# Layer-norm transposes by DMA instead of TensorE, with the second normalization after the attention output

## What is computed

```python
# attention, on xn = layernorm(x)
q = softmax(xn @ Wq, axis=-1)
k = softmax(xn @ Wk, axis=-2)
v = xn @ Wv
ctx = (k.T @ v) / 8            # 1024 x 1024 per sequence
x = x + ((q @ ctx) / 1024) @ Wo + bo

# mixture of experts, on h = layernorm(x)
probs = sigmoid((h @ Wr) * routing_bias)        # 7 routed experts
scores, idx = top_k(probs, 2); scores /= scores.sum(-1)
out = shared_expert(h) + sum_e expert_e(h) * weight_e
expert(h) = (silu(h @ wg) * (h @ wu)) @ wd      # 1024 -> 2816 -> 1024
x = x + out
```

## Time and profile before

| | |
|---|---|
| device time, two timed runs | 4908.41 and 4373.74 us, median 4641.08 us |
| device time of the profiled execution | 4353.71 us |
| its span on the slowest core (core 5) | 4352.2 us |
| spans of all cores | 4312.2 to 4352.2 us |
| first expert matmul | 669.4 us |

### The profile page before, as it was taken

One profiled execution on the slowest core, in us unless ns is written; L12 is line 12 of the kernel. 1 busy time (PEld: TensorE's weight loads), 2 busy tenths in 40 slices (PEclk: granted clock), 3 DMA queues, 4 the chain that ended last, 5 costly groups with the idle time before them and its releaser, 6 DMA issues.

```text
span 4352.2 us, 48589 instructions; the slowest of 8 cores (4312.2 to 4352.2 us)
## 1 busy us (share of the span) xinstructions
PE 4134.2 (95%) x19072; PEld 1879.8 (43%) x19072; DVE 944.8 (22%) x1314; ACT 530.6 (12%) x930; POOL 235.8 (5%) x269
## 2 busy tenths in 40 slices
PE   5899548999999999999999999999999999999998
PEld 2344223444444444444444444444444444444443
DVE  2111331222222221212221222222222222122212
ACT  2211111011110101010101010101111010101010
POOL 1000220000000000000000000000000000000000
PEclk7789768999999999999999999999999999999999
DMA  6001104222130313131313131222222130213132
GB/s 121 24 0 25 49 20 66 37 39 42 26 55 15 55 21 49 30 51 27 53 23 54 27 49 32 44 37 39 42 35 46 17 63 15 47 29 49 27 54 78
DMA packets 83199, 175.64 MB, mean 40 GB/s; under 512 B 5024, under 2 KB 5024, under 8 KB 82976
## 3 DMA queue, kind: packets, MB, share of 16 engines
q0 software_dynamic: 76288, 147.36, 21.6%
q1 hardware_dynamic: 6688, 25.17, 1.8%
HBM read 310.94 MB, written 8.39 MB: 73 GB/s over the span
## 4 chain that ended last, share of the span: by engine, by line
PE 95%; DVE 2%; issue 1%; POOL 1%; ACT 1%; DMA 1%; DVEq 0%; POOLq 0%; ACTq 0%; SPq 0%
PE PS L520 28%; PE PS L529 28%; PE PS L554 14%; PE PS L556 14%; PE PS L273 2%; PE PS L248 1%; PE PS L374 1%; PE PS L454 1%; PE PS L456 1%; PE PS L301 1%; PE PS L297 1%; PE PS L295 1%; PE PS L299 1%; PE PS L323 1%; PE PS L325 1%
## 5 line engine op out<-in xcount | busy, mean ns | idle before, releaser
L520 PE MATMUL PS<-h2T,ring 128*128 128x512 bf16 x5632 | 1332.1, 379 | 10.9 <-DMA ring<-wgu 10.9
L529 PE MATMUL PS<-h2T,ring 128*128 128x512 bf16 x5632 | 1331.4, 379 | 0.0
L554 PE MATMUL PS<-wd_sb,hid 128*128 128x512 bf16 x2816 | 1067.2, 379 | 16.8 <-DVE hid L539 16.8
L556 PE MATMUL PS<-wd_sb,hid 128*128 128x512 bf16 x2816 | 1067.2, 379 | 0.0
L539 DVE TENSOR_TENSOR hid<-sg,PS 128x512 bf16<-128x512 bf16 x704 | 484.2, 688 | 1950.2 <-PE PS L529 1950.2
L520 PEld LDWEIGHTS PS<-h2T,ring 128*128 128x128 bf16 x5632 | 551.3, 98 | 676.2 <-issue 12.7
L529 PEld LDWEIGHTS PS<-h2T,ring 128*128 128x128 bf16 x5632 | 551.3, 98 | 665.6 <-issue 1.9
L536 ACT ACTIVATE sg<-PS 128x512 bf16<-128x512 f32 x704 | 420.5, 597 | 3165.1 <-PE PS L520 3165.0
L562 DVE SCALAR_TENSOR_TENSOR x<-PS,w_sb,x 128x1024 f32<-128x1024 f32 x224 | 287.6, 1284 | 801.3 <-PE PS L556 801.3
L554 PEld LDWEIGHTS PS<-wd_sb,hid 128*128 128x128 bf16 x2816 | 275.4, 98 | 354.8 <-issue 24.2
L556 PEld LDWEIGHTS PS<-wd_sb,hid 128*128 128x128 bf16 x2816 | 275.4, 98 | 330.3
(11 more groups left out here) (71 smaller groups left out, 821.4 us busy)
## 6 DMA issues: line engine op xcount, KB each, us to landing
ring<-wgu POOLq DMA_DIRECT2D x176, 512.0 KB, 5.4
wd_sb<-rdn POOLq DMA_DIRECT2D x14, 1536.0 KB, 15.1
wd_sb<-rdn POOLq DMA_DIRECT2D x14, 1280.0 KB, 16.5
xslot<-x SPq DMA_DIRECT2D x32, 512.0 KB, 3.7
out<-x SPq DMA_DIRECT2D x2, 4096.0 KB, 13.0
wd_sb<-sdn POOLq DMA_DIRECT2D x2, 1536.0 KB, 15.5
wd_sb<-sdn POOLq DMA_DIRECT2D x2, 1280.0 KB, 16.3
wq_sb<-wq POOLq DMA_DIRECT2D x1, 2048.0 KB, 22.6
```

What stands on the lines that cost most here:

```text
L520: last = te.matmul(PSUM[:, gb * 512:(gb + 1) * 512], ring[slot][:, 0, ic, :], h2T[:, ic, noff:noff + 512], start=(ic == 0), stop=(ic == NI ...
L529: last = te.matmul(PSUM[:, ub * 512:(ub + 1) * 512], ring[slot][:, 1, ic, :], h2T[:, ic, noff:noff + 512], start=(ic == 0), stop=(ic == NI ...
L554: last = te.matmul(PSUM[:, b0 * 512:(b0 + 1) * 512], lhs, wd_sb[wbuf][:, hcl, 0:512], start=st, stop=sp_)
L556: last = te.matmul(PSUM[:, b1 * 512:(b1 + 1) * 512], lhs, wd_sb[wbuf][:, hcl, 512:1024], start=st, stop=sp_)
```

## The change

- The eight TensorE transposes and two ScalarE evictions of `layernorm_transpose` are replaced by one DMA transpose on the SP queue, from the scratch tile straight into h1T or h2T. The scratch tiles become bf16. A resource, `xp_chain`, makes each transpose wait for the completion of the one before.
- In `layernorm_transpose` VectorE computes veps ahead of negm.
- The interleaved loop is taken apart: first the attention output for all 16 tiles, then `snap_a8` and the allocation of the expert buffers, then, in four blocks, the normalization of four tiles followed by the routing of four tiles.
- In `emit_routing` the last step, one operation with two multiplications, becomes two operations, and the banks are 4 and 5.

```diff
-    h1scr = alloc("h1scr", [128, D], F32, side="right")
+    h1scr = alloc("h1scr", [128, D], BF16, side="right")
...
+    xp_chain = Res()
...
+    s_xp = p.sem("s_xp")
...
         p.op("dve", lambda v: v.bn_aggr(mv[:], stat6[:]), reads=[stat_r], writes=[mv_r])
+        p.op("dve", lambda v: v.tensor_scalar(veps[:], mv[:, 1:2], EPS, None, ALU.add),
+             reads=[mv_r], writes=[veps_r])
         p.op("dve", lambda v: v.tensor_scalar(negm[:], mv[:, 0:1], -1.0, None, ALU.mult),
              reads=[mv_r], writes=[negm_r])
-        p.op("dve", lambda v: v.tensor_scalar(veps[:], mv[:, 1:2], EPS, None, ALU.add),
-             reads=[mv_r], writes=[veps_r])
...
              reads=[src_res, negm_r, rstd_r], writes=[scr_res])
-        for half in range(2):
-            bank = banks[half]
-
-            def tfn(te, half=half, bank=bank):
-                last = None
-                for q in range(4):
-                    ic = half * 4 + q
-                    last = te.transpose(PSUM[:, bank * 512 + q * 128: bank * 512 + (q + 1) * 128],
-                                        scr[:, ic * 128:(ic + 1) * 128], ident[:])
-                return last
-            p.op("pe", tfn, reads=[scr_res, ident_r], writes=[PS[bank]])
-
-            def efn(e, half=half, bank=bank, t=t):
-                dst = dstT[:, half * 4:(half + 1) * 4, t * 128:(t + 1) * 128]
-                src = PSUM[:, bank * 512:(bank + 1) * 512]
-                return e.activation(dst, src, AF.Copy)
-            p.op("act", efn, reads=[PS[bank]], writes=[dstT_res])
+        p.op("sp", lambda sp, t=t: sp.dma_start_transpose(
+            dstT[:, 0:8, t * 128:(t + 1) * 128], scr[:]),
+            reads=[scr_res, xp_chain], writes=[dstT_res, xp_chain],
+            sem=s_xp, inc=16)
...
-    def emit_routing(t, bank=None):
-        if bank is None:
-            bank = 4 if t % 2 == 0 else 5
+    for t in range(NT):
...
+    free("xb1"); free("xb0"); free("bo_bc"); free("wo_sb"); free("yT")
+    snap_a8 = p.snapshot()
...
+    def emit_routing(t):
+        bank = 4 if t % 2 == 0 else 5
...
+        p.op("dve", lambda v: v.tensor_scalar(wtmp[:, 0:NR], probs[:, 0:NR], minv[:],
+                                              None, ALU.mult),
+             reads=[probs_r, minv_r], writes=[wtmp_r])
...
-        p.op("dve", lambda v, t=t: v.scalar_tensor_tensor(
-            w_sb[:, t * 8: t * 8 + NR], probs[:, 0:NR], minv[:], maskb[:, 0:NR],
-            ALU.mult, ALU.mult),
-            reads=[probs_r, minv_r, mask_r], writes=[w_r])
...
-    h2scr = alloc("h2scr", [128, D], F32, side="right")
-    h2scr_r = Res(war0=snap_a7)
-
-    def emit_ln2_routing(t):
-        layernorm_transpose(t, x2[:, t * D:(t + 1) * D], x2_r[t], h2scr, h2scr_r,
-                            h2T, h2T_r[t // 4], banks=(4, 5) if t % 2 == 0 else (6, 7))
-        emit_routing(t, bank=7 if t % 2 == 0 else 5)
...
-        if t >= 2:
-            emit_ln2_routing(t - 2)
-    for t in (NT - 2, NT - 1):
-        emit_ln2_routing(t)
...
+        p.op("dve", lambda v, t=t: v.tensor_tensor(
+            w_sb[:, t * 8: t * 8 + NR], wtmp[:, 0:NR], maskb[:, 0:NR], ALU.mult),
+            reads=[wtmp_r, mask_r], writes=[w_r])
+
+
+    h2scr = alloc("h2scr", [128, D], BF16, side="right")
+    h2scr_r = Res(war0=snap_a8)
+    for blk in range(NT // 4):
+        for t in range(blk * 4, blk * 4 + 4):
+            layernorm_transpose(t, x2[:, t * D:(t + 1) * D], x2_r[t], h2scr, h2scr_r,
+                                h2T, h2T_r[t // 4], banks=(0, 1) if t % 2 == 0 else (2, 3))
+        for t in range(blk * 4, blk * 4 + 4):
+            emit_routing(t)
+    free("h2scr")
```

More of the change, by code:

```diff
@@ L466, in build_nc @@
             reads=[PS[b0], PS[b0 + 1], rsq_r, xb_r[sl]], writes=[x2_r[t]])
-        if t >= 2:
-            emit_ln2_routing(t - 2)
-    for t in (NT - 2, NT - 1):
-        emit_ln2_routing(t)
-    free("h2scr"); free("xb1"); free("xb0"); free("bo_bc"); free("wo_sb"); free("yT")
+    free("xb1"); free("xb0"); free("bo_bc"); free("wo_sb"); free("yT")
     snap_a8 = p.snapshot()
@@ L485, in build_nc, with lfn @@
     sg_r = [Res(war0=snap_a8), Res(war0=snap_a8)]
+    def emit_routing(t):
+        bank = 4 if t % 2 == 0 else 5
+        def lfn(te, t=t, bank=bank):
+            last = None
+            for ic in range(NI):
+                last = te.matmul(PSUM[:, bank * 512: bank * 512 + NR],
+                                 h2T[:, ic, t * 128:(t + 1) * 128],
+                                 wr_sb[:, ic, :], start=(ic == 0), stop=(ic == NI - 1))
+            return last
+        p.op("pe", lfn, reads=[h2T_r[t // 4], wr_r], writes=[PS[bank]])
+        p.op("dve", lambda v, bank=bank: v.tensor_tensor(
+            wtmp[:, 0:NR], PSUM[:, bank * 512: bank * 512 + NR], rb_bc[:], ALU.mult),
+            reads=[PS[bank], rb_r], writes=[wtmp_r])
+        p.op("act", lambda s: s.activation(maskb[:, 0:NR], wtmp[:, 0:NR], AF.Exp,
+                                           scale=-1.0),
+             reads=[wtmp_r], writes=[mask_r])
+        p.op("dve", lambda v: v.tensor_scalar(maskb[:, 0:NR], maskb[:, 0:NR], 1.0,
+                                              None, ALU.add),
+             reads=[mask_r], writes=[mask_r])
+        p.op("dve", lambda v: v.reciprocal(probs[:, 0:NR], maskb[:, 0:NR]),
+             reads=[mask_r], writes=[probs_r])
+        p.op("dve", lambda v: v.max(m8[:], probs[:]), reads=[probs_r], writes=[m8_r])
+        p.op("dve", lambda v: v.tensor_tensor(msum[:], m8[:, 0:1], m8[:, 1:2], ALU.add),
+             reads=[m8_r], writes=[msum_r])
+        p.op("dve", lambda v: v.reciprocal(minv[:], msum[:]), reads=[msum_r], writes=[minv_r])
+        p.op("dve", lambda v: v.tensor_scalar(wtmp[:, 0:NR], probs[:, 0:NR], minv[:],
+                                              None, ALU.mult),
+             reads=[probs_r, minv_r], writes=[wtmp_r])
+        p.op("dve", lambda v: v.tensor_scalar(maskb[:, 0:NR], probs[:, 0:NR], m8[:, 1:2],
+                                              None, ALU.is_ge),
+             reads=[probs_r, m8_r], writes=[mask_r])
+        p.op("dve", lambda v, t=t: v.tensor_tensor(
+            w_sb[:, t * 8: t * 8 + NR], wtmp[:, 0:NR], maskb[:, 0:NR], ALU.mult),
+            reads=[wtmp_r, mask_r], writes=[w_r])
```

## The result

| | before | after |
|---|---|---|
| device time | 4317 to 4318 us, one of 4374 | 4358 to 4366 us |
| ratio of device times, 95% interval | 1 | 1.0102, 1.0089 to 1.0114 |
| profiled execution's span, core 3 | 4312.2 us | 4361.5 us |

The changed kernel is 1.0% slower, about 44 us. Every kernel here also has executions that are up to hundreds of microseconds longer at a lower granted clock: they are left out of all device times and ratios, and where a kernel gave no other, the span of one of its cores at the usual clock is given instead.

The account below looks back on a forecast made before the run. Outside the TensorE-busy expert loop, chains through one tile were taken to bound the two changed pieces. First stage +84 and second -30 gave +54 on 4353.71, so 4408 us; range 4340 to 4540.

Parts of the forecast that it names:

- the base: The undisturbed time of the kernel before, to which the predicted difference was added: the profiled execution's 4353.71 us.
- T: Time from issue of a 128x1024 bf16 DMA transpose to its landing: taken as 5 us, between 2.6 and 14.8.
- the formula: Whole kernel's predicted difference, -70 + 12I + 20T: +54 us with I = 2 and T = 5.
- I: Time SP is held between issuing a transpose and issuing what is behind it: taken as 2 us, at least 0.33.
- within 2%: Whole kernel: time changes by less than 2%, about what a measurement was taken to tell from no change; chance 0.57.
- The x load loses its prefetch and lies on the chain: First normalization: the next x load queues behind the transpose on SP; a tile takes 8.2 + I = 10.2 us, not 4.83.
- First stage +84: First normalization and Q matmuls, four blocks: a loss of 40.4 + 12I + 4T = 84 us.
- Second stage -30: Attention output, second normalization and routing, up to the experts: a gain of 110.3 - 16T = 30 us.
- the 7.85 us wait: Before the experts: the wait for first expert weights, claimed covered by issuing them during the last transpose and routing.
- Attention output alone at 3.46 us a tile: Second stage's start: TensorE sets the pace without transposes, 16 x 3.46 = 55.4 us.
- The rival at 0.81: Attention output alone: runs at the lower clock or paced by POOL, 13 us more; inside the forecast's range, no separate chance.
- price of its small pieces: Each of 32 transposes pays per small piece: T = 10.5 gives 4534 us, T = 14.8 gives 4660; chance 0.38.

Follow-up runs that it names:

- e1: The changed kernel with each x load of the first normalization issued ahead of the transpose of the tile before: 4306 us, 0.9973 of before.
- e5: The kernel before, TensorE transposes kept, with each x load of the first normalization issued only once the tile before is normalized: 4372 us, 1.0127 of before.
- e7: The changed kernel with each transpose split into two DMA transposes of 512 columns, the second waiting for the first: core 1 spans 4419.6 us.
- e4: The changed kernel with the first expert weights issued only when the last transpose has landed: 4349 us, timed once.
- e6: The changed kernel with the loads of Wk and Wv issued only after the first four transposes have landed: core 1 spans 4347.0 us, no device time.
- e8: The kernel before with next-block normalization between Q matmuls (TensorE transposes) and a rearranged interleaved second stage with DMA transposes, first expert weights behind the last: 4196.6 us.
- e10: The kernel of e8 with msum, a sum of two 128x1 columns on VectorE, written as tensor_scalar instead of tensor_tensor: 4191.2 us, timed once.

## Why the prediction was right and where it was wrong

The forecast was 4408 us, the changed kernel takes 4361. Of the 47 us between them 36 are the base (item 9): against the 4318 us that the kernel before takes, the forecast says +90 where +44 was measured. The other 10 are the sum, +54 against +44. That it came so near is luck: its term T was 5 us where 3.07 was measured, which by the formula (20T) is 39 us too much, and I, 2 us where 1.37 was measured, is 8 us too much (12I). With both as measured the formula gives +8; delays that it did not contain make up for most of the difference (items 4 and 5). The time is inside the range, and "within 2%" holds. But the text took 2% as what a measurement can tell, and this one told 1.0% from none, with an interval of 0.12% to either side: a sum of +1.2% should have been called slower.

1. *The x load loses its prefetch and lies on the chain.* Right; e1 and e5 show it from both sides, and e5's tile of 8.19 us on core 4 is the forecast's 8.2 without I.
2. *T.* Forecast 5 us, measured 3.07: the term that was mis-sized most. 1024 small pieces are indeed packets (the queue table of after has 33,792 more packets on q1 than the earlier trace rows for 32 transposes, 1056 each), but the price of 0.197 us did not apply to them: by e7 the 32 pieces per engine of 512 columns cost 0.67 us, 21 ns each. The step of the sum that failed is this term: 5 us were chosen between 2.6, a plain copy, and 14.8, the price per packet, and that price was read from packets that are 1.9 KB on average. A price per packet taken from larger packets is no price for small ones.
3. *I.* Forecast 2 us, measured 1.37 (88.15 to 89.52).
4. *First stage +84, measured +91 on core 3, 84 to 87 on five others.* With the measured T and I the formula gives 40.4 + 16.4 + 12.3 = 69 us, so two errors hid each other. What it left out is that a load is slower beside a transpose: in the first block a load of 20.8 us where 8.8 was taken, Q from 69.3 instead of 59.3 (33.0 and the formula's 26.3); later, loads of 4.1 to 5.5 us where 3.65 was taken, 8.6 us for the nine on core 3's chain.
5. *Second stage -30, measured -41.* With T = 3.07 the formula gives -61. 13 of the missing 20 are the last transpose beside the first weights. The text named the 7.85 us wait as covered by earlier weight loads and did not ask what the earlier transfers would hit: they hit the transpose that went out with them. Of the rest, a block's routing and the restart behind it take 14.8 us, three times (landing at 563.54, 560.48 and 3.06, to POOL at 578.36), where 13.7 was counted, and in the kernel before core 3 took 1.7 us less for this stage than core 5, which was read.
6. *Attention output alone at 3.46 us a tile.* Right: 55.8 us at a clock of 1.00. The rival at 0.81 did not come.
7. *The expert loop unchanged.* Right, within 1.1 us.
8. *POOL's write in bf16 at 1.19 us.* Right, 1.19.
9. *The base.* The forecast added its difference to 4353.7 us, an execution whose core 5 had the clock of 0.81 for the K/V stage. This is the step that moved the forecast most. The text saw the 0.81 and carried it as if it were the kernel's. On core 5 the stages from K/V to yT take 265.3 us (167.0 to 432.3) where core 3 needs 237.1, and the blocks before them 10 us more. Cores 0 to 3 of the same profile stood at 4312 to 4317, and against 4318 the same difference gives 4372 instead of 4408.

Beside the rival "price of its small pieces" stood a figure of the Trainium skill (VectorE: DVE Perf Modes, The three transpose paths): 1309 ns for a 128x128 square. Measured, eight squares in one DMA take 3.07 us, not the 10.5 of that estimate, so its time is not the number of squares times 1309 ns; the measurement decides. A piece beside the weight loads is another matter. The Trainium skill (DMA: Bandwidth & Descriptors, Queues, rings and completion order) says that a DMA engine goes round its queues packet by packet. If each of an engine's 64 pieces waited for one packet of the weights as the trace counts them, that would be 64 x 0.197 = 12.6 us on top of 3.07, or 15.7; measured are 16.2 to 19.5. But the Trainium skill has some 9 to 17 descriptors in one such packet, and if its packets are not those that the trace counts, there are fewer turns. e4 and e6 show that the delay comes and goes with the weight loads. That it comes by turns is not shown by a run.

## What to carry to other kernels

When a transfer that waits for computed data is put on an in-order queue, look at what is queued behind it: here the next tile's load, and moving it one place ahead was worth 55 us. A transfer of many small pieces is cheap alone and several times dearer beside a bulk load, so a bulk load that becomes free to start earlier should be checked for what it will run beside. A change of two halves is best costed as two: one of these was worth 56 us and the other cost 99.

## What the runs showed of the hardware

- A DMA transpose of 128x1024 bf16 within the core lands in 3.07 us, one of 512 columns in 2.4; SP is held 1.22 and 1.17 us.
- The same transpose takes 16.2 us beside 2.5 MB of weight loads (core 3; 14.6 to 18.4 on the others) and up to 19.5 beside the loads of Wq, Wk and Wv (core 1 of e1).
- A load of x takes 8.3 to 9.0 us beside those weights (e5, core 1) and 21.1 with a transpose issued 1.7 us ahead of it (after, core 1).
- Small VectorE operations waited for a POOL operation to end: a 128x1 tensor_tensor took 1.3 us on average instead of 0.16 (e8), a 128x7 tensor_scalar 1.22 instead of 0.21 (e10). The two operations between them in e10, a 128x1 tensor_scalar and a reciprocal, took 0.21 and 0.16 us beside the same POOL addition. The Trainium skill (SBUF — State Buffer, SBUF: two separate sides) says that VectorE, with two SBUF inputs or in a faster mode that uses two ports, and GpSimd hold a shared pair of ports in turn for a whole instruction. The trace agrees for the tensor_tensor; which mode the tensor_scalar ran in no run here shows.
